# The prologue of an adaLN cross-attention kernel in a new order, with turned modulations and values placed by DMA

## The chip, the cores and the metric

The kernel runs on one core of a Trainium2 chip. The metric is the device time of one execution in microseconds (us). TensorE multiplies matrices, VectorE, ScalarE and GpSimd work elementwise, SyncE (SP) issues transfers. The engines run their own instruction streams and wait for each other by semaphores.

## The reference

```python
def _ada_ln(x, c, W_ss, b_ss):
    h = (x - mean(x)) / sqrt(var(x) + EPS)
    scale, bias = jnp.split(jax.nn.silu(c) @ W_ss + b_ss, 2, axis=-1)
    return (1.0 + scale)[:, None, :] * h + bias[:, None, :]
...
xq, xkv = _ada_ln(x_q, t_vec, Wss_q, bss_q), _ada_ln(x_kv, t_vec, Wss_kv, bss_kv)
q = (xq @ Wq + bq).reshape(B, Lq, nh, dh)          # 16 x 1024 x 512, 16 heads of 32
kv = (xkv @ Wkv + bkv).reshape(B, Lkv, 2, nh, dh)  # 64 context rows per batch
attn = softmax(q k^T / sqrt(dh));  out = attn v
return x_q + (out @ Wp + bp)
```

## The kernel before

There are 16 batches of 1024 rows; a unit is 128 rows, so there are 128 units, eight to a batch. Every matrix product is done in parts: an operand is split into a high and a low half-precision (or fp32r) part, and high x high, high x low and low x high are summed. The scales for these parts come from upper bounds, the limits, worked out at run time.

All engines run `prime()` and then `step(b, i)` for every unit, by `every_step`. A step of TensorE is score(i), turn_p(i-2), project(i+4), turn_x(i+8), project_out(i-3), weigh(i-2); the pipeline is full from the step of unit 3 on. The prologue, `prime()` and what stands ahead of it, does the work that is there only once:

- the small vectors are turned (L1025, L1027), silu of the condition is formed (L719 to L728), and `modulate` (L1032) multiplies it with Wss_kv and Wss_q, 512 columns streamed at a time; ScalarE copies the rows (L495), TensorE turns them (L1043), VectorE adds the biases (L747)
- VectorE makes statistics of the context rows (L735) and normalises them in `cx` (L755); TensorE turns them chunk by chunk (L1053), VectorE scales and shifts a chunk (L964, L967), ScalarE makes its high part (L629), GpSimd its low part (L357)
- ScalarE sums squares of the weights; `limits`, `limits_top`, `limits_copy` and `scales` (L757 to L816) make all scales from one table of 16 limits, through a transpose and a spreading product on TensorE (L1221, L1224)
- `value_rows(t)` and `key_rows(n)` (L1085, L1092) are 12 products each, eight tiles of both. A value tile's parts are formed in one go (L700 ScalarE, L833 VectorE) in `v16`, and `place` (L265) copies them to `v_all` with four copies on each engine. A key tile goes by L823, L690, L439
- `turn_x` (L1118) turns the first x tiles, which ScalarE and GpSimd have normalised (L576, L583, L370, L373, L385); Wq is scaled in four pieces (L408, L591, L951); `project` (L1135) makes the first queries, in the banks ps_q and ps_o; `bias_product` (L1106) makes the output bias; `shift_product` (L1060) the query's
- key tile 7 is made last, behind the projections. Wp's parts are made in steps 0 and 1 (L624, L937)

What sets the order is the order written in each engine's `prime()`, and the waits on semaphores in it. SP issues loads in the order of its stream and waits in it for free buffers.

## Time and profile before

| what | value |
|---|---|
| three runs | 1185.43, 1185.86, 1186.97 us, median 1185.86 |
| the profiled execution | 1185.47 us, of which the span is 1183.7 us |
| instructions | 32530 |
| busy in the span | TensorE 1140.7, VectorE 1019.2, ScalarE 858.0, GpSimd 840.1 us |
| mean granted TensorE clock | 0.986 |
| first score / fourth score start | 119.01 / 147.28 us |
| key tile 3 of 8 ends | 73.3 us |
| silu finished on VectorE | 6.04 us |
| L349 and L351 on GpSimd, four tiles' reciprocal roots | 19.43 to 20.74 us |
| a square of 128x2048 weights on ScalarE (L642) | 1.91 us |
| the limits' power on GpSimd (L445) | 1.01 us |
| scale steps L788 to L805 on VectorE | 48.42 to 50.72 us, of it 1.12 in one step of four elements |
| sums of one x tile's rows on ScalarE (L576, L583) | 1.47 us from start to start |

A profile row tells an engine's busy time, the mean of one instruction and what ended the idle time before it. TensorE instructions overlap, so the distance of two starts tells their pace better than their length. The granted clock is 1.0 at 2.4 GHz and 0.5 at 1.2 GHz.

### The profile page before, as it was taken

Reading aid. Unit: us, or ns where it says so; the run is one execution under the profiler, and the core shown is the slowest. Engines: PE = TensorE matmul, PEld = TensorE weight load, DVE = VectorE, ACT = ScalarE, POOL = GpSimd, SP = SyncE. Lnnn points to the kernel's source line nnn. Section 1 sums busy time; section 2 is a strip of 40 time slices with the busy share of each in tenths; the row PEclk is TensorE's granted clock in tenths of the full one; section 3 lists DMA queues with packets and bytes.
Section 4 is the critical chain, followed back from the end, with each engine's and each line's share of the span. In section 5 each row is a group of like instructions: output and inputs, shape, how many; then the busy total and the mean of one; then the engine's idle time right before and its main releaser. Section 6 shows DMA issues by size and latency. Waiting matters only on the chain.

```text
span 1183.7 us, 32530 instructions
## 1 busy us (share of the span) xinstructions
PE 1140.7 (96%) x11072; PEld 696.6 (59%) x11072; DVE 1019.2 (86%) x1799; ACT 858.0 (72%) x1624; POOL 840.1 (71%) x941
## 2 busy tenths in 40 slices
PE   7798699999999999999999999999999999999997
PEld 2665366566665666656666566566665666656653
DVE  4745698989989889898898988989889899898895
ACT  2477577778777777777777777777787777787653
POOL 1543486877778786868787786868687777869555
PEclk9798799999999999999999999999999999999999
DMA  8111113223223232232322323223232232232222
GB/s 331 70 36 36 63 64 100 99 90 106 89 97 106 80 106 90 96 106 80 106 92 94 106 80 106 97 89 106 81 105 97 90 106 86 100 107 65 72 73 80
DMA packets 59871, 112.00 MB, mean 95 GB/s; under 512 B 6412, under 2 KB 6440, under 8 KB 59832
## 3 DMA queue, kind: packets, MB, share of 16 engines
q1 hardware_dynamic: 59832, 111.48, 27.6%
q8 instruction: 24, 0.39, 0.1%
q14 instruction: 15, 0.12, 0.0%
HBM read 77.90 MB, written 33.55 MB: 94 GB/s over the span
## 4 chain that ended last, share of the span: by engine, by line
PE 86%; issue 2%; POOL 2%; ACT 1%; DVE 0%; POOLq 0%; ACTq 0%; DVEq 0%
PE ps_q L1135 27%; PE ps_o L1203 26%; PE ps_t L1169 11%; PE ps_v L1188 8%; PE ps_s L1154 8%; PE ps_v L1118 4%; POOL xr L418 1%; PE ps_o L1135 0%; POOL xr L394 0%; PE ps_v L1082 0%; POOL half_den L425 0%; POOL xh L385 0%; PE ps_t L1118 0%; DVE xT_lo L847 0%; ACT xT_hi L510 0%
## 5 line engine op out<-in xcount | busy, mean ns | idle before, releaser
L394 POOL TENSOR_TENSOR xr<-xr,bp_row 128x512 f32<-128x512 f32 x128 | 163.1, 1274 | 155.9 <-ACT junk L583 155.9
L885 DVE TENSOR_REDUCE mx<-ps_s 128x8 f32<-128x512 f32 x256 | 164.8, 685 | 90.8 <-PE ps_s L1154 90.4
L425 POOL TENSOR_TENSOR half_den<-pr 128x512 f32<-128x512 f32 x128 | 162.8, 1272 | 64.6 <-ACT pr L612 35.0
L558 ACT CAST pt_hi<-ps_t 128x512 f16<-128x512 f32 x256 | 137.6, 589 | 92.5 <-PE ps_t L1169 92.5
L568 ACT ACTIVATE q_hi<-ps_q,cur_bq 128x512 f16<-128x512 f32 x126 | 86.5, 687 | 133.0 <-PE ps_q L1135 110.1
L418 POOL TENSOR_TENSOR xr<-y,xr 128x512 f32<-128x512 f32 x128 | 162.4, 1269 | 6.5 <-ACT y L535 6.5
L905 DVE TENSOR_TENSOR pt_lo<-ps_t,pt_hi 128x512 f16<-128x512 f32 x256 | 163.3, 679 | 0.0
L877 DVE SCALAR_TENSOR_TENSOR pr<-pr,ps_v 128x512 f32<-128x512 f32 x256 | 162.8, 675 | 0.0
L897 DVE TENSOR_TENSOR pr<-ps_s,mx 128x512 f32<-128x512 f32 x256 | 161.9, 673 | 0.0
L612 ACT ACTIVATE pr<-pr,exp_scale 128x1024 f32<-128x1024 f32 x128 | 146.4, 1144 | 16.4 <-DVE pr L897 16.4
L1169 PE MATMUL ps_t<-ident,pr 128*128 128x128 f32 x1024 | 140.9, 281 | 4.7 <-DVE pr L877 4.7
L1203 PE MATMUL ps_o<-wp_hi,oT_hi 128*128 128x512 f16 x512 | 131.5, 379 | 6.7 <-DVE oT_lo L854 6.7
L1135 PE MATMUL ps_q<-xT_hi,w_hi 128*128 128x512 f16 x504 | 131.1, 383 | 2.1 <-DVE q_lo L915 1.8
L1203 PE MATMUL ps_o<-wp_lo,oT_hi 128*128 128x512 f16 x512 | 131.4, 379 | 0.0
L1203 PE MATMUL ps_o<-wp_hi,oT_lo 128*128 128x512 f16 x512 | 131.4, 379 | 0.0
L1135 PE MATMUL ps_q<-xT_lo,w_hi 128*128 128x512 f16 x504 | 130.6, 382 | 0.0
L1135 PE MATMUL ps_q<-xT_hi,w_lo 128*128 128x512 f16 x504 | 130.2, 381 | 0.0
L1169 PEld LDWEIGHTS ps_t<-ident,pr 128*128 128x128 f32 x1024 | 110.3, 142 | 18.4 <-DVE pr L877 5.2
L1188 PEld LDWEIGHTS ps_v<-pt_hi,vb 128*64 128x64 f16 x2048 | 82.4, 109 | 55.8 <-issue 55.8
L1154 PE MATMUL ps_s<-kb,q_hi 64*128 64x128 f16 x2048 | 108.0, 217 | 0.2 <-DVE pr L897 0.2
L1188 PE MATMUL ps_v<-pt_hi,vb 128*64 128x128 f16 x2048 | 103.0, 222 | 1.7 <-DVE xT_lo L847 1.7
L535 ACT ACTIVATE y<-ps_o,y_unscale 128x512 f32<-128x512 f32 x128 | 88.1, 688 | 18.2 <-PE ps_o L1203 14.6
(162 smaller groups left out, 2292.7 us busy)
## 6 DMA issues: line engine op xcount, KB each, us to landing
x_in<-in_x_dram SPq DMA_DIRECT2D x128, 256.0 KB, 2.7
xr<-in_x_dram SPq DMA_DIRECT2D x128, 256.0 KB, 2.9
out_dram<-xr SPq DMA_DIRECT2D x128, 256.0 KB, 2.0
raw<-in_L_xcond_Wss_kv_dram SPq DMA_DIRECT2D x4, 512.0 KB, 5.0
cx<-in_ctx_dram SPq DMA_DIRECT2D x1, 2048.0 KB, 12.1
raw<-in_L_xcond_Wss_q_dram SPq DMA_DIRECT2D x4, 512.0 KB, 12.8
raw<-in_L_xcond_Wkv_dram SPq DMA_DIRECT2D x2, 1024.0 KB, 15.9
wq<-in_L_xcond_Wq_dram SPq DMA_DIRECT2D x1, 1024.0 KB, 16.5
```

What stands on the lines that cost most here:

```text
L394: pool.tensor_tensor(xr[:, s, :], xr[:, s, :], bp_row[:, :], ALU.add).then_inc(xr_ready, 1)
L418: pool.tensor_tensor(xr[:, s, :], y[:, off % 2, :], xr[:, s, :], ALU.add).then_inc(y_ready, 1)
L425: pool.tensor_tensor(half_den[:, :, :], pr[:, off % 2, :, 0:LKV // 2], pr[:, off % 2, :, LKV // 2:LKV], ALU.add).then_inc(half_done, 1)
L877: dve.scalar_tensor_tensor(out=pr[:, off % 2, hs, :], in0=pr[:, off % 2, hs, :], scalar=P_UNIT, in1=rden[:, hs].unsqueeze(2).to_broadcast( ...
L885: dve.tensor_reduce(mx[:, HALF * h:HALF * (h + 1)], ps_s[:, h, :].rearrange("p (h l) -> p h l", l=LKV), AX_X, ALU.max)\
L897: dve.tensor_tensor(pr[:, off % 2, hs, :], ps_s[:, h, :].rearrange("p (h l) -> p h l", l=LKV), mx[:, hs].unsqueeze(2).to_broadcast([P, HAL ...
L905: dve.tensor_tensor(pt_lo[:, 4 * h:4 * h + 4, :], ps_t[:, h, :].rearrange("p (g n) -> p g n", g=4), pt_hi[:, 4 * h:4 * h + 4, :], ALU.subt ...
L1135: last = pe.matmul(bank[:, :], w[:, k, cols], xt[:, s, k, :], start=(n == 0), stop=(n == 3 * KC - 1))
L1154: last = pe.matmul(ps_s[:, e, P * m:P * (m + 1)], q[rows, s, m, cols], kb[rows, part, m, :, :].rearrange("p h l -> p (h l)"), start=(n == ...
L1169: last = pe.transpose(ps_t[:, h, P * g:P * (g + 1)], pr[:, off % 2, 2 * pair:2 * pair + 2, :].rearrange("p h l -> p (h l)"), ident[:, :])
L1188: last = pe.matmul(ps_v[64 * e:64 * (e + 1), 0, P * m:P * (m + 1)], vb[:, part, 2 * m + e, :, :].rearrange("p h c -> p (h c)"), pt[:, 4 * ...
L1203: last = pe.matmul(ps_o[:, :], ot[:, k, :], w[:, k, :], start=(n == 0), stop=(n == 3 * KC - 1))
```

## The change

- Modulation: the product is formed turned, 128x128 pieces of Wss as weights and the 16 columns of silu streamed, so that the copies L495 and the turns L1043 go. Wss_q gets a tile of its own, the loads of Wss come by columns. The first modulation follows three turned chunks; the second comes after key tile 0.
- Loads: the small vectors are issued by ScalarE's queue; SP's begin with half of the context, in two-tile pieces, then Wss_kv, Wv, the rest of the context, Wk, Wq, Wss_q, Wp, x.
- Limits: two stages of 8, one for keys and values, one for query and output, each with its transpose, spreading product and scale steps.
- Context rows 4 to 7 are normalised by GpSimd. The first four x tiles get their statistics and their rows on VectorE (`first_stats`, `first_rows`) and are turned from `x_in`.
- Values: parts are written by parity of heads, two instructions on each engine, and four DMAs per tile from SP (`place_values`) take the place of the eight copies.
- Weights' high parts are made in halves and low parts in quarters. `value_rows` and `key_rows` wait for each piece and use listed banks, partly those of the loop.
- All value and key tiles are done before the loop; three of each come after the projections.
- `step` is the same but for waits.

```diff
+            return ps_t[:, off % 2, :] if isinstance(b, int) and unit(b, off) < PER else ps_v[:, 0, :]
...
+        def chunk_bank(n):
+
+            return (ps_t[:, 0, :], ps_t[:, 1, :], ps_q[:, :])[n % TURNED]
+
+        def value_bank(t):
+
+            return (ps_s[:, 0, :], ps_s[:, 1, :], ps_v[:, 0, :], ps_v[:, 1, :], ps_v[:, 0, :], ps_t[:, 0, :],
+                    ps_t[:, 0, :], ps_o[:, :])[t]
+
+        def key_bank(n):
+
+            return (ps_s[:, 0, :], ps_s[:, 1, :], ps_v[:, 0, :], ps_v[:, 1, :], ps_v[:, 1, :], ps_t[:, 1, :],
+                    ps_t[:, 1, :], ps_o[:, :])[n]
...
+            load_context(0)
+            load_context(1)
+            load_modulation(0, Wss_kv, ld_ss)
             sp.dma_start(wv_raw, Wkv[:, H:2 * H].rearrange("(k p) n -> p k n", p=P)).then_inc(ld_wv, 16)
+            load_context(2)
+            load_context(3)
+            sp.dma_start(wk_raw, Wkv[:, 0:H].rearrange("(k p) n -> p k n", p=P)).then_inc(ld_wk, 16)
             sp.dma_start(wq[:, :, :], Wq.rearrange("(k p) n -> p k n", p=P)).then_inc(ld_wq, 16)
-            sp.dma_start(wk_raw, Wkv[:, 0:H].rearrange("(k p) n -> p k n", p=P)).then_inc(ld_wk, 16)
-            sp.dma_start(bp_row[:, :], bp.rearrange("(a n) -> a n", a=1).partition_broadcast(P)).then_inc(ld_bp, 16)
+            load_modulation(1, Wss_q, ld_ssq)
+            sp.dma_start(wp_raw, Wp.rearrange("(k p) n -> p k n", p=P)).then_inc(ld_wp, 16)
 
...
-                wait(sp, xh_ready, unit(b, off - 3))
+                if isinstance(b, int) and FIRST <= unit(b, off) < 2 * FIRST:
+                    wait(sp, xT_turned, unit(b, off - 3))
+                wait(sp, xh_ready, nth(b, off - 3))
...
+            def place_values(t):
+
+                sp.wait_ge(v_lo_done, 2 * t + 2)
+                for hb in range(2):
+                    for par in range(2):
+                        sp.dma_start(v_all[LKV * par:LKV * (par + 1), :, 2 * t + hb, :, :],
+                                     v16[LKV * hb:LKV * (hb + 1), :, t % 2, par, :]
+                                     .rearrange("p s (g d) -> p s g d", d=DH)).then_inc(v_placed[t % 2], 16)
...
+            sp.dma_start(bp_row[:, :], bp.rearrange("(a n) -> a n", a=1).partition_broadcast(P)).then_inc(ld_bp, 16)
+            for t in range(4):
+                place_values(t)
+            load_x(0, 4)
+            load_x(0, 5)
+            place_values(4)
+            for f in range(6, 12):
                 load_x(0, f)
+            for t in range(5, CT):
+                place_values(t)
...
+                context_rstd(1)
+                context_rows(4)
+                context_rows(5)
+                limits(0)
+                context_rows(6)
+                context_rows(7)
+                for n in range(KC, 2 * KC):
+                    context_lo(n)
+                key_lo(0)
+                first_rstd()
+                key_lo(1)
+                limits(1)
+                key_lo(2)
+                for m in range(KC):
+                    scaled_wq(0, m)
+                    if m == 1:
+                        key_lo(3)
+                layernorm(4)
+                layernorm(5)
+                key_lo(4)
                 layernorm(6)
                 layernorm(7)
...
+            act.dma_start(c_row, cond).then_inc(ld_small, 16)
+            for at, v, n in ((BSSQ, bss_q, 2 * KC), (BSSKV, bss_kv, 2 * KC), (BQ, bq, KC), (BK, bkv, 2 * KC)):
+                act.dma_start(brow[at:at + n, :], v.rearrange("(r c) -> r c", c=P)).then_inc(ld_small, 16)
...
-            for side in range(2):
-                act.wait_ge(mod_mm, side + 1)
-                banks = (ps_s, ps_v)[side]
-                act.copy(mod_rows[side].rearrange("b (a n) -> b a n", a=2), banks[0:B, :, :]).then_inc(mod_copied, 1)
...
+                context_hi(0)
+                value_weights_hi(0)
+                context_hi(1)
+                value_weights_hi(1)
+                context_hi(2)
+                context_hi(3)
+                sum_of_squares(wv_raw, ld_wv, 0, 1, squares[0])
+                sum_of_squares(wk_raw, ld_wk, 0, 0, squares[0])
+                key_weights_hi(0)
+                key_weights_hi(1)
+                act.wait_ge(wv_done, KC)
+                sum_of_squares(wq[:, :, :], ld_wq, 1, 0, squares[1])
+                for n in range(KC):
+                    value_hi(n)
+                    context_hi(KC + n)
+                key_hi(0)
+                sum_of_squares(wp_raw, ld_wp, 1, 1, squares[1])
+                for n in range(1, KC):
+                    key_hi(n)
+                    if n == 2:
+                        scaled_wq_hi(0, 0)
+                scaled_wq_hi(0, 1)
+                act.wait_ge(wv_done, KC)
...
-                    act.wait_ge(lim_step, SCALED_SC)
-                wait(act, v_lo_done, t - 1)
-                wait(act, v_hi_placed, t - 1)
-                act.activation(v16[0][:, t % 2, :], ps_s[:, t % 2, :], ACT.Copy, scale=v_scale[:, 0:1])\
...
-            def value_hi_place(t):
-
-                act.wait_ge(v_hi_done, t + 1)
-                place(act.copy, 0, t).then_inc(v_hi_placed, 1)
+                    act.wait_ge(kv_step, V_SCALED)
+                wait(act, v_placed[t % 2], 64 * (t // 2))
+                heads = value_bank(t).rearrange("p (g e d) -> p g e d", e=2, d=DH)
+                for par in range(2):
+                    act.activation(v16[:, 0, t % 2, par, :].rearrange("p (g d) -> p g d", d=DH), heads[:, :, par, :],
+                                   ACT.Copy, scale=v_scale[:, 0:1]).then_inc(v_hi_done, 1)
...
+                for n in range(KC):
+                    context_chunk(n)
+                    if n > 0:
+                        value_weights_lo(n - 1)
+                value_weights_lo(3)
+                context_stats(1)
+                limits(0)
+                limits_top(0)
+                key_weights_lo(0)
+                key_weights_lo(1)
+                limits_copy(0)
+                key_weights_lo(2)
+                key_value_scales()
+                key_weights_lo(3)
+                for n in range(KC):
+                    value_lo(n)
+                    context_chunk(KC + n)
+                modulation(1)
+                limits(1)
+                keys(0)
+                first_stats()
+                keys(1)
+                limits_top(1)
+                first_rows(0)
+                first_rows(1)
+                keys(2)
+                limits_copy(1)
+                first_rows(2)
+                first_rows(3)
+                query_output_scales()
+                query_bias()
+                keys(3)
+                first_wq_lo(0)
+                turned_x(0, 0)
+                first_wq_lo(1)
+                turned_x(0, 1)
+                turned_x(0, 2)
+                first_wq_lo(2)
+                turned_x(0, 3)
+                output_bias()
+                first_wq_lo(3)
+                value_lo(4)
+                query(0, 0, first_banks[0])
+                turned_x(0, 4)
+                keys(4)
+                query(0, 1, first_banks[1])
+                turned_x(0, 5)
+                query(0, 2, first_banks[0])
+                turned_x(0, 6)
+                query(0, 3, first_banks[1])
+                turned_x(0, 7)
+                for n in range(5, CT):
+                    value_lo(n)
+                    keys(n)
 
...
-                for k in range(KC):
-                    pe.wait_ge(landed[k], 16)
-                    for a in range(2):
-                        last = pe.matmul((ps_s, ps_v)[side][0:B, a, :], silu_t[:, k, :],
-                                         wss[side][:, k, H * a:H * (a + 1)], start=(k == 0), stop=(k == KC - 1))
+                dst = (ps_v[:, 1, :], ps_o[:, :])[side]
+                for m in range(2 * KC):
+                    pe.wait_ge(landed[m // 2], 16)
+                    for k in range(KC):
+                        last = pe.matmul(dst[:, B * m:B * (m + 1)], wss[side][:, k, P * m:P * (m + 1)],
+                                         silu_t[:, k, :], start=(k == 0), stop=(k == KC - 1))
                 last.then_inc(mod_mm, 1)
 
-            def turn_modulation(side):
-                pe.wait_ge(mod_copied, side + 1)
-                for m in range(2 * KC):
-                    last = pe.transpose(ps_t[:, side, B * m:B * (m + 1)], mod_rows[side][:, P * m:P * (m + 1)],
-                                        ident[0:B, 0:B])
-                last.then_inc(mod_turned, 1)
-
...
+                for n in range(TURNED):
+                    turn_context(n)
+                modulate(0, ld_ss)
+                turn_context(3)
                 value_rows(0)
...
+                value_rows(1)
+                limits_turn(0)
+                value_rows(2)
+                limits_spread(0)
+                value_rows(3)
+                for n in range(KC, 2 * KC - 1):
+                    turn_context(n)
                 key_rows(0)
...
+                pe.wait_ge(lim_copied, 1)
+                modulate(1, ld_ssq)
+                turn_context(2 * KC - 1)
+                key_rows(1)
+                pe.wait_ge(mod_ready, 4)
+                limits_turn(1)
+                key_rows(2)
+                limits_spread(1)
+                pe.wait_ge(ld_wq, 16)
+                pe.wait_ge(c_mul, CT)
+                for m in range(KC):
+                    shift_product(m)
+                key_rows(3)
+                for f in range(FIRST):
+                    turn_x(0, f)
+                value_rows(4)
+                bias_product()
+                pe.wait_ge(bq_ready, 1)
+                for m in range(KC):
+                    if m == 1:
                         pe.wait_ge(bias_ready, 1)
-                        project(0, 0, first_banks[0], 1)
-                for m in range(1, KC):
                     project(0, m, first_banks[m % 2], 1)
-                    turn_x(0, KC + m)
-                key_rows(CT - 1)
+                    turn_x(0, FIRST + m)
+                    if m == 0:
+                        key_rows(4)
+                for t in range(5, CT):
+                    value_rows(t)
+                    key_rows(t)
 
```

## Rows read from the trace of the kernel before

**Rows 1.** Stretches: busy us (and instructions) of TensorE, its loads, VectorE, ScalarE, GpSimd; clock; DMA.
```profile
0.00:26.90 26.90, 18.46 (x57) 5.34 (x57) 11.62 (x36) 4.55 (x5) 3.61 (x16) 1.00 0.88 326
26.90:52.40 25.50, 18.14 (x87) 15.46 (x88) 19.68 (x41) 13.81 (x17) 13.17 (x9) 0.73 0.33 122
52.40:119.00 66.60, 60.44 (x257) 41.39 (x255) 35.58 (x71) 47.83 (x108) 26.18 (x36) 0.95 0.11 32
119.00:147.28 28.28, 18.78 (x153) 10.35 (x153) 19.40 (x30) 15.76 (x29) 13.49 (x19) 0.76 0.20 66
```
**Rows 2.** The chain of waits in order of time: start, us, what; two scores in the loop.
```profile
147.35 0.78 PE ps_s L1154 x24
...
155.56 0.78 PE ps_s L1154 x24
```
**Rows 3.** Timeline of VectorE: start, us, line, operation: statistics and first chunks.
```profile
16.50 2.47 DVE L735 BATCH_NORM_STATS2 cst<-cx 128x6 f32<-128x512 f32 x4 [10.46 <-DMA cx<-in_ctx_dram]
...
19.16 2.44 DVE L735 BATCH_NORM_STATS2 cst<-cx 128x6 f32<-128x512 f32 x4
...
22.37 3.73 DVE L755 TENSOR_SCALAR cx<-cx,cmv,crstd 128x512 f32<-128x512 f32 x8
...
26.92 0.68 DVE L964 TENSOR_TENSOR raw<-ps_t,sc_kv 128x512 f32<-128x512 f32 x1
...
28.25 0.68 DVE L964 TENSOR_TENSOR raw<-ps_t,sc_kv 128x512 f32<-128x512 f32 x1
```
**Rows 4.** Transfers by line: size, median us from issue to landing.
```profile
raw<-in_L_xcond_Wss_kv_dram SPq DMA_DIRECT2D x4, 512.0 KB, 5.0
```
**Rows 5.** Timeline of TensorE: turned chunks and 16-column products, at either clock.
```profile
28.83 0.96 PE L1060 MATMUL ps_q<-sh_q,wq 128*128 128x16 f32 x8
29.65 0.64 PE L1053 MATMUL ps_t<-ident,cx 128*128 128x128 f32 x4
...
34.26 1.12 PE L1053 MATMUL ps_t<-ident,cx 128*128 128x128 f32 x4 [3.18 <-DVE raw L964]
35.17 1.73 PE L1060 MATMUL ps_q<-sh_q,wq 128*128 128x16 f32 x8
36.74 1.09 PE L1053 MATMUL ps_t<-ident,cx 128*128 128x128 f32 x4
```
**Rows 6.** Timeline of TensorE's weights loads, in the first modulation.
```profile
8.63 0.15 PEld L1036 LDWEIGHTS ps_s<-raw,silu_t 128*16 128x16 f32 x1 [0.70 <-issue]
9.49 0.15 PEld L1036 LDWEIGHTS ps_s<-raw,silu_t 128*16 128x16 f32 x1 [0.70 <-issue]
10.03 0.10 PEld L1036 LDWEIGHTS ps_s<-raw,silu_t 128*16 128x16 f32 x1 [0.40 <-issue]
10.46 0.10 PEld L1036 LDWEIGHTS ps_s<-raw,silu_t 128*16 128x16 f32 x1 [0.33 <-issue]
```
**Rows 7.** Groups by line up to 147.3 us: count, busy us, mean ns, idle before.
```profile
L265 ACT COPY v_all<-pt_hi 64x256 f16<-64x256 f16 x32 | 12.9, 402 | 0.3
L833 DVE SCALAR_TENSOR_TENSOR pt_lo<-ps_s,v_scale,pt_hi 128x512 f16<-128x512 f32 x8 | 6.0, 744 | 6.4 <-ACT pt_hi L700 6.4
L629 ACT CAST ctx_hi<-raw 128x512 fp32r<-128x512 f32 x8 | 4.9, 614 | 9.4 <-DVE raw L967 9.4
```
**Rows 8.** Timeline of TensorE: the start of a key tile, the output bias behind it.
```profile
55.19 1.09 PE L1082 MATMUL ps_v<-ctx_hi,wk_hi 128*128 128x512 f32 x4
...
57.98 3.60 PE L1106 MATMUL ps_o<-xr,o_slot 128*128 128x512 f32 x8
61.02 1.49 PE L1082 MATMUL ps_s<-wv_hi,ctx_hi 128*128 128x512 f32 x4
```
**Rows 9.** Timeline of TensorE while the loop's pipeline fills.
```profile
138.53 1.97 PE L1169 MATMUL ps_t<-ident,pr 128*128 128x128 f32 x8 [4.56 <-DVE pr L877]
```
**Rows 10.** Timeline of GpSimd and of VectorE, two instructions at once.
```profile
43.65 2.85 POOL L357 TENSOR_TENSOR ctx_lo<-raw,ctx_hi 128x512 fp32r<-128x512 f32 x1 [4.23 <-ACT ctx_hi L629]
...
45.60 0.92 DVE L778 TENSOR_SCALAR lim_diag<-ident,lim_top 16x16 f32<-16x16 f32 x1
```

634 lines of the change are left out of this document (315 added, 319 removed).

## The prediction

> **What bounds the kernel now.** First the stretches of the whole trace, stage by stage. TensorE is busy without a gap once the loop runs; in front of it the row of stretches shows the share it loses [rows 1]: 8.4 us of the first 26.9, 7.4 us of the next 25.5, 6.2 us of the 66.6 up to the first score, and 9.5 us of the 28.3 in which the pipeline of the loop fills. Beside the gaps stands the granted clock: 0.73 in the second stretch and 0.76 in the last. Second the chain of waits: from 146.5 us on it is TensorE alone, and a score comes every 8.21 us to the end [rows 2]. The change leaves those steps alone, so whatever it does must show as a shift of the moment at which the fourth score, score(0, 3), starts. That is 147.28 us now. All I have to work out is this moment in the new order.
>
> **Stage 1, to the end of modulation 0 (call it M), the one for keys and values.** Now the context arrives behind the weights of the modulation and its statistics start at 16.5 us; chunk 0 of the context is scaled at 26.92 us [rows 3]. In the new order the context comes first. 512 KB from the head of the queue land 5.0 us after their issue in the median [rows 4], and the vector pass over two tiles can start at about 6.3 us, once VectorE has finished the silu steps, which precede it. Four tiles of statistics take 2.66 us, as the distance of the two groups shows [rows 3]; the power on GpSimd is about 1.4 us with its waits and four normalised rows are four times 0.47 us. That puts the last of them at 12.4 us, and TensorE, idle since 4.5 us, starts the three turns there.
>
> Here I chose with care, since this is the largest term. Nothing new is computed in the modulation, but it changes shape: eight columns of four 128x128 weights loads with 16 columns streamed, instead of 512 columns streamed past a 16-column weight. The old one cannot price it. The query's shift product L1060 has exactly the new shape, 16 columns, four k. At the high clock one m takes 0.82 us (28.83 to 29.65), at the low one 1.57 us (35.17 to 36.74); a turned chunk takes 0.91 us at the low one (34.26 to 35.17) [rows 5]. So one modulation is 8 x 0.82 = 6.6 us at 2.4 GHz and 8 x 1.57 = 12.6 us at 1.2 GHz. Which clock? The clock column says 1.00 for the first stretch, but the rows say otherwise: the weights loads of the first modulation come 0.86 us apart up to 9.49 and 0.43 us apart after 10.03 [rows 6]. TensorE began at the low level although the column does not say so, and left it after 3.9 us of streaming 512 columns at a time. The stretch 34.3 to 37.8 us is made of just what the new order has at 12.4 to 27 us, turned chunks and 16-column products, and it stayed at the low level to its end [rows 5]. I take the low level for all of it: three turns end at 14.5 us (the first one is nearly finished when the last row is), plus 12.6 gives M = 27.1. Lower end: the clock rises as it did in the old modulation, some 4 us into the work, M = 21.6. What the new form removes, the two ScalarE copies of 1.0 us and the second transposes, is paid for by this: chunk 0 starts at 27.1 + 0.35 = 27.5 us against 26.92.
>
> **Stage 2, to the end of key tile 3 (K3).** TensorE waits for others here, so I followed the hand-written order on all engines; times are counted from M.
>
> Each chunk takes VectorE 1.33 us [rows 3], ScalarE's high part 0.61 [rows 7]. Four chunks with the halves and quarters of the value weights between them end at M+7.4, the last low part on GpSimd at M+9.4. Value tile 0 then ends at M+11.9 and tile 1, half of it at the low clock, at M+15.2; a tile is 2.79 us at the high clock [rows 8].
>
> The first limit waits for two squares on ScalarE (M+12.0) and for tile 1; TensorE's order puts tile 2 between turning and spreading. Spread at M+18.4, power 1.0, the six steps and v_scale 1.9: M+21.3.
>
> Then ScalarE and VectorE alternate: high part of a value tile 0.8, low part 0.8, chunk 1.36, its high part 0.55, none beside another: 3.55 us x 4 (halves cost a little more than the 0.74 us of a whole [rows 7]), and 0.6 us for chunk 7, whose turn is queued behind the second modulation on TensorE: M+36.1.
>
> keys(0), its high part and the square of Wp put the second limit at M+40.8, 4.7 later. Key tile 2, the spread (0.3), four 16-column products (3.3) and key tile 3: M+50.0. The change adds waits on SP: loads of x tiles 4 to 11 stand behind placements. ScalarE asks for x tile 4 some 8 us after its load lands, and value_hi(2) asks for the place of tile 0 some 6 us after its low part, for four issues and a landing of about 4.5; both are covered, and cost up to 3 us if a placement took twice that.
>
> To this I add 0.8 us for the port that VectorE and GpSimd share, bounded below. K3 = 27.1 + 50.8 = 77.9. Now key tile 3 ends at 73.3.
>
> **Stage 3, K3 to the first score.** Left are four value and four key tiles (8 x 2.78 = 22.2), the output bias 3.05 us [rows 8], four projections at 2.6 (10.4) and eight turned x tiles at 0.4 (3.3): 39.0 us. The four x tiles turn in two banks and each waits for VectorE and ScalarE between the pieces of Wq: 5.0 us idle, value tile 4 then runs mostly at the low clock, 1.6 more, and key tile 7 shares ps_o with value tile 7 and waits 1.5 us for its low part. 39.0 + 8.0 = 47.0; first score at 124.9, now 119.0. What leaves ScalarE (placing: 32 copies, 12.9 us [rows 7]) does not shorten this, as TensorE is the one that is late in it.
>
> **Stage 4, filling.** Unchanged code, but ScalarE, VectorE and GpSimd come to it less burdened: now q_hi of the fifth query waits for x rows of GpSimd, which stood behind key_lo(7). With that gone project(0, 5) comes 1.5 us and the first normalised tile 2.4 us earlier. TensorE's wait of 4.56 us before it [rows 9] stays in kind, since wp_hi and wp_lo are still in the way. 28.3 - 2.4 = 25.9.
>
> **Sum.** 124.9 + 25.9 = 150.8 against 147.28: +3.5 us. The profiled execution took 1185.47 us (1183.7 of span and 1.8 around it), 0.4 below the median 1185.86. 1185.5 + 3.5 = **1189.0 us**.
>
> **Rivals.** First, *the clock rises in the modulation.* M = 21.6; the rest follows it, as nothing in stage 2 waits for a load. 5.5 us less: 1183.5 us. For it: the old modulation did rise. Against: it streamed 512 columns, and the turned chunks and 16-column products at 34.3 us did not. The Trainium skill, TensorE: Matmul & The Clock Gate, PE-mode transpose, adds that transposes do not count as activity for the gate; no run here shows them alone. Chance 0.2.
>
> Second, *it works as a reordering should.* The clock rises, and stage 3 runs warm with the turned x tiles hidden: 5.5, and 5 of the 8 us lost in stage 3: 1178.5 us. For it: 12.9 us of copies leave ScalarE, and four tiles' row sums, 1.5 us each. Against: the written order, which chains x tiles to pieces of Wq. Chance 0.15.
>
> Third, *GpSimd in the way of VectorE.* The new order moves four context rows onto GpSimd, next to the limit steps and weights parts on VectorE. The row of GpSimd at 43.65 took 2.85 us where its like took 1.27 without company, and VectorE's 16-element step that began at 45.60 lasted 0.92 us until it ended [rows 10]. If every one of the eight low parts and four rows costs 0.5 to 1.6 us on the chained path and the clock falls inside the second modulation too, that is 5 us more: 1194 us. It decides once two such steps in each of the four rounds collide. The Trainium skill, SBUF — State Buffer, Who interferes with whom, makes it a lock held for a whole instruction whenever VectorE has two SBUF inputs; every second step of a chunk has. Bounded: 0 below (no meeting), 6 above; I took 0.8. Chance 0.15.
>
> **Numbers.** Forecast 0.5 (its own range 1186 to 1193), of which about 0.15 lies within 0.2% of the median, 1183.5 to 1188.2 us, about what a measurement can tell from no change. Rival 1 is half in that band, half below. Faster 0.1 + 0.15 = 0.25, same 0.15 + 0.1 = 0.25, slower 0.35 + 0.15 = 0.5. The range 1180 to 1195 leaves out the lower half of rival 2 and the upper third of rival 3, with the ends of the forecast's own.
>
> **What would show it.** Modulation 0 between 14.5 and 27 us with weights loads twice as far apart as after the clock has risen; its rows 0.1 us apart instead of 0.2 would mean rival 1. chunk 0 at 27.5, last chunk at 63, key tile 3 done at 78, first score at 125, fourth at 151, loop steps still 8.21 us. The prediction is wrong if loop steps change, or if TensorE does not wait for VectorE between 31 and 68 us.

## The result, and the profile after

The changed kernel takes 1201.92 us in the median (1199.72 to 1204.59), the kernel before in the same comparison 1186.41: ratio 1.0131, interval 1.0108 to 1.0154, 15.5 us slower. The forecast was 1189.0, range 1180 to 1195: the sign holds, the size doesn't, and the time lies outside the range. The profiled execution took 1199.72 us, its span 1197.9. It is the fastest of the four, so the traces below explain 14.2 of the 15.5 us.

First the chain of waits after, two scores in the loop (start, us, what), then the stretches of the trace, cut where the prediction's four stages end (columns as in [rows 1]):

```profile
161.57 0.78 PE ps_s L1323 x24
...
169.78 0.78 PE ps_s L1323 x24
```

```profile
0.00:32.30 32.30, 17.61 (x81) 16.69 (x81) 6.65 (x20) 1.54 (x2) 2.30 (x15) 1.00 0.99 342
32.30:88.90 56.60, 46.22 (x218) 37.76 (x219) 38.64 (x92) 21.89 (x32) 29.05 (x23) 0.91 0.11 33
88.90:136.80 47.90, 41.79 (x185) 28.60 (x183) 17.89 (x29) 22.63 (x50) 15.30 (x22) 0.96 0.22 65
136.80:161.50 24.70, 15.47 (x153) 9.67 (x152) 19.16 (x30) 17.08 (x32) 12.02 (x16) 0.86 0.23 78
```

A score still comes every 8.21 us [rows 2]. The fourth starts 14.2 us later than before (161.5, was 147.3), and from it to the end of the span it is 1036.4 us in both kernels, and within 0.2 us of that in each one below. So a kernel can be judged by the start of its fourth score, and the stages can be set against the sum:

| stage | forecast | after |
|---|---|---|
| 1, to the end of modulation 0 (M) | 27.1 | 32.3 |
| 2, M to the end of key tile 3 | 50.8 | 56.6 |
| 3, to the first score | 47.0 | 47.9 |
| 4, first to fourth score | 25.9 | 24.7 |

Stages 3 and 4 are right within 1.2 us. TensorE's timeline after shows what became of the first two (in brackets the idle time before, and what ended it):

```profile
8.15 0.28 PE L1160 MATMUL ps_t<-ident,o_slot 28*128 28x28 f32 x1 [8.15 <-DMA o_slot<-in_L_xcond_bkv_dram]
...
15.34 2.61 PE L1182 MATMUL ps_t<-ident,cx 128*128 128x128 f32 x8 [6.51 <-DVE cx L841]
...
18.59 13.67 PE L1172 MATMUL ps_v<-silu_t,raw 128*128 128x16 f32 x64
...
58.45 0.33 PE L1182 MATMUL ps_t<-ident,cx 128*128 128x128 f32 x1 [1.91 <-POOL cx L401]
...
62.28 8.74 PE L1172 MATMUL ps_o<-silu_t,wss_q_raw 128*128 128x16 f32 x64
70.86 1.09 PE L1182 MATMUL ps_t<-ident,cx 128*128 128x128 f32 x4
71.61 2.06 PE L1253 MATMUL ps_s<-ctx_hi,wk_hi 128*128 128x512 f32 x4
...
77.50 0.27 PE L1197 MATMUL ps_o<-ident,lim 128*8 128x128 f32 x1 [1.54 <-issue]
...
80.90 3.75 PE L1189 MATMUL ps_q<-sh_q,wq 128*128 128x16 f32 x32
84.49 1.84 PE L1253 MATMUL ps_v<-ctx_hi,wk_hi 128*128 128x512 f32 x4
```

The first row: the small vectors are there at 8.15 us, before it was 3.7, and TensorE is idle until then. Modulation 0 takes 13.67 us, all at the low level: 0.21 us a product, where eight products with the clock up take 0.81 us (62.84 to 63.65 in a7 below). Behind value tile 3 a turn waits 1.91 us for a row of GpSimd; modulation 1 and the shift products end with the clock down, and key tiles 1 and 3 (71.61, 84.49) begin at 1.2 GHz, as 2.06 and 1.84 us for four products show where 1.1 is the length at the high clock [rows 8]. The turn of the second limit (77.50) starts when the square of Wp is finished on ScalarE:

```profile
75.40 1.91 ACT L572 ACTIVATE raw<-xr 128x2048 f32<-128x2048 f32 x1
77.21 0.19 ACT L572 ACTIVATION_READ_ACCUMULATOR raw<-xr 128x1 f32 x1
```

GpSimd's timeline after, the context rows that it took over:

```profile
46.70 4.16 POOL L401 TENSOR_SCALAR cx<-cx,cmv,crstd 128x512 f32<-128x512 f32 x2
...
54.08 4.31 POOL L401 TENSOR_SCALAR cx<-cx,cmv,crstd 128x512 f32<-128x512 f32 x2
```

And the alternation behind them, on ScalarE and on VectorE: a high part of a chunk, two halves of a value tile, then the low halves and the next chunk, 3.6 us a round:

```profile
60.26 0.62 ACT L708 CAST ctx_hi<-raw 128x512 fp32r<-128x512 f32 x1 [3.48 <-DVE raw L1074]
60.79 0.83 ACT L791 ACTIVATE v<-ps_s,v_scale 128x256 f16<-128x256 f32 x2
63.89 0.62 ACT L708 CAST ctx_hi<-raw 128x512 fp32r<-128x512 f32 x1 [2.27 <-DVE raw L1074]
```

```profile
61.65 0.88 DVE L929 SCALAR_TENSOR_TENSOR v<-ps_s,v_scale,v 128x256 f16<-128x256 f32 x2 [1.43 <-ACT v L791]
62.45 0.68 DVE L1071 TENSOR_TENSOR raw<-ps_q,sc_kv 128x512 f32<-128x512 f32 x1
63.16 0.69 DVE L1074 TENSOR_TENSOR raw<-raw,sh_kv 128x512 f32<-128x512 f32 x1
```

The first chunks show one thing more. While GpSimd makes low parts (first line, the next one from 39.52 on), VectorE's steps with both inputs in SBUF take 1.37, 1.03 and 1.31 us where the same steps take 0.68 or 0.69 without company:

```profile
34.84 3.40 POOL L415 TENSOR_TENSOR ctx_lo<-raw,ctx_hi 128x512 fp32r<-128x512 f32 x2 [20.22 <-ACT ctx_hi L708]
35.74 1.37 DVE L1078 TENSOR_TENSOR wv_lo<-raw,wv_hi 128x512 fp32r<-128x512 f32 x1 [0.30 <-ACT wv_hi L713]
37.75 1.03 DVE L1074 TENSOR_TENSOR raw<-raw,sh_kv 128x512 f32<-128x512 f32 x1
40.02 1.31 DVE L1074 TENSOR_TENSOR raw<-raw,sh_kv 128x512 f32<-128x512 f32 x1
```

### The profile page after: what moved, and what is told of

It reads as the page before. It is cut to its first block, busy times and chain, and to the rows that moved or that the text cites. A ratio compares the mean times of both kernels' runs of the same rounds, so it can differ in the third digit from the quotient of the medians.

```text
span 1197.9 us, 32905 instructions
## 1 busy us (share of the span) xinstructions
PE 1146.0 (96%) x11155; PEld 716.9 (60%) x11155; DVE 1015.4 (85%) x1796; ACT 839.9 (70%) x1584; POOL 844.6 (71%) x937
## 4 chain that ended last, share of the span: by engine, by line
PE 83%; issue 3%; POOL 1%; DVE 0%; ACT 0%; POOLq 0%; DVEq 0%
PE ps_q L1302 26%; PE ps_o L1372 26%; PE ps_t L1339 10%; PE ps_v L1356 8%; PE ps_s L1323 8%; PE ps_v L1285 4%; POOL xr L476 1%; POOL xr L452 0%; POOL half_den L483 0%; ACT wp_hi L703 0%; DVE mx L993 0%; POOLq L42 0%; DVE den L970 0%; DVE pr L1005 0%; ACT pr L692 0%
## 5 line engine op out<-in xcount | busy, mean ns | idle before, releaser
L610 ACT ACTIVATE y<-ps_o,unscale 128x512 f32<-128x512 f32 x128 | 88.2, 689 | 18.2 <-PE ps_o L1372 14.9
## 6 DMA issues: line engine op xcount, KB each, us to landing
raw<-in_L_xcond_Wkv_dram SPq DMA_DIRECT2D x2, 1024.0 KB, 11.4
wss_q_raw<-in_L_xcond_Wss_q_dram SPq DMA_DIRECT2D x4, 512.0 KB, 11.4
```

## The experiments

Kernels are called by the first part of their names (a1, b2): those with an a start from the changed kernel, those with a b from the kernel before. The median of the kernel before lay between 1185.1 and 1186.4 us in the comparisons; the ratio stands with each kernel. "Fourth score" is of its profiled execution.

**One term of the new kernel at a time.** a1, small vectors at the head of SP's stream again:

```diff
-            act.dma_start(c_row, cond).then_inc(ld_small, 16)   # and brow, on ScalarE's queue
+            sp.dma_start(c_row, cond).then_inc(ld_small, 16)    # and brow, ahead of load_context(0)
```

> The changed kernel with one edit: the five small vectors go back to the head of SP's stream, in front of the context. Theory (the loss is a sum of waits on one chain through the prologue): the vectors landed at 8.15 us where they landed at 3.7 before, silu, statistics and all behind them shift by that; the fourth score, at 161.5 us in the changed kernel, comes at about 157.3, 4.2 us earlier, and the time falls by as much. Rival (slack behind it: the loads of Wss_kv or the weights squares set the next waits): less than 1 us, fourth score at 160.5 or later.

Measured: 1197.25 us, 1.0102 (1.0083 to 1.0120). Vectors at 3.78, modulation 0 from 14.30 to 27.98: the 4.3 us came. The fourth score of the profile came only 2.5 earlier (159.0), since modulation 1 now took 9.5 us and the tiles behind it more of the low clock.

a3, context rows 4 to 7 on VectorE instead of GpSimd:

```diff
-                context_rows(4) ... context_rows(7)     # pool
+                for t in range(4, CT): dve.tensor_scalar(cx[:, t, :], ...)   # behind limits(0)
```

> The changed kernel with context rows 4 to 7 normalised by VectorE behind the first limits, not by GpSimd. Theory (GpSimd needs 2.1 us for a row where it took 0.77 for an x row before, and chunk 4 waits 2.2 us for them): chunk 4 no longer waits, VectorE spends 1.9 us more in a stretch where it waits for the limit anyway; fourth score at about 159.5, 2 us earlier. Rival (the rows ran beside other waits): within 0.5 us of 161.5.

Measured: 1200.82 us, 1.0136 (1.0119 to 1.0154). Chunks 4 to 6 turn without a wait and key tile 0 starts at 57.55 instead of 59.4, but modulation 1 then takes 9.88 us instead of 8.74, and the fourth score comes at 160.4: nothing that the times can tell. The row itself was mis-sized: 2.08 us on GpSimd, where its like, with an addition in place of the subtraction, takes 0.89 in the mean in the kernel before. VectorE was idle from 45.8 to 49.7 us, over most of the first pair, so for this pair it isn't the meeting of the two engines on their shared port.

a2, products of 512 columns on junk ahead of the turns and of modulation 0, to raise the clock first:

```diff
+            warm(12)        # before the small vectors
+            warm(26)        # before pe.wait_ge(silu_step, 3)
```

> The changed kernel with 12 and 26 extra matmuls of 512 columns into an unused bank, ahead of the small turns and ahead of the first turned chunks, where TensorE waits anyway. Theory (modulation 0 took 13.7 us because TensorE was at 1.2 GHz): it runs like modulation 1, 8.7 us, and the three turned chunks in 1.6 instead of 3.2; 6.4 us earlier by its end, fourth score at about 155.5. Rival (the form is bound by its weights loads at either clock): modulation 0 stays above 12 us, fourth score at 160 or later.

Measured: 1199.74 us, 1.0121 (1.0098 to 1.0145). Modulation 0 took 10.79 us, not 13.67, and key tile 0 started 4.9 us earlier; modulation 1 then took 11.15 us and the fourth score came at 162.3, 0.8 later than without. The gain up to key tile 0 was given back.

a4, chunk 7's turn ahead of modulation 1:

```diff
+                turn_context(2 * KC - 1)
                 modulate(1, ld_ssq)
-                turn_context(2 * KC - 1)
```

> The changed kernel with chunk 7 turned ahead of modulation 1 instead of behind it. Theory: VectorE's wait of 2.2 us for that chunk goes, but the end of modulation 1 comes 0.5 us later and key tile 1 behind it; the second limit waits for the square of Wp, which follows chunk 7's high part and keys(0), so it comes 2 us earlier; fourth score at about 159.7. Rival (TensorE's key tile 1, not the chunk, sets the second limit): 161.5, no change.

Measured: 1201.17 us, 1.0136 (1.0109 to 1.0163), no gain: limit 2 is turned at 77.1 us (77.5 after), so chunk 7 wasn't what it waited for.

**Is it TensorE's work at all?** a6, modulation 1 with one of its four k, so that three quarters of its sum are left out:

```diff
-                    for k in range(KC):
+                    for k in range(KC if side == 0 else 1):
...
```

> The new kernel with modulation 1 cut to one of its four k: 8 products instead of 32, so three quarters of its sum are left out. It took 8.74 us, so 6.5 us of TensorE's work go, and nothing is moved. Theory one, TensorE is the bound from value tile 1 to key tile 3, with products of 16 columns that lose it the clock: chunk 7 no longer waits 2.2 us for its turn, and limit 2, shift products and key tile 3 come 5 to 6 us earlier, with key tile 1 at the high clock. First score at 131.5 instead of 136.8, time 1196. Theory two, the alternation of ScalarE and VectorE with GpSimd's rows is the bound and TensorE only follows: only chunk 7's wait of 2.2 us goes, first score at 134.6, time 1199.7 or more.

Measured: 1201.01 us, 1.0133 (1.0115 to 1.0151). 6.9 us of work are gone and nothing is gained. Its timeline of TensorE says where they went:

```profile
62.80 1.85 PE L1172 MATMUL ps_o<-silu_t,wss_q_raw 128*128 128x16 f32 x16
...
74.16 0.37 PE L1197 MATMUL ps_o<-ident,lim 128*8 128x128 f32 x1 [6.22 <-ACT raw L572]
74.28 2.04 PE L1253 MATMUL ps_v<-ctx_hi,wk_hi 128*128 128x512 f32 x4
```

TensorE waits 6.22 us for L572, the square of Wp, which ScalarE does behind the alternation, and comes out of the wait at the low clock: key tile 2, the shift products and key tile 3 take 15.1 us instead of 11.3. The limit is turned 3.3 us earlier than with all four k (74.16, was 77.50), and the clock takes 3.8 back. Both theories expected a gain; both missed this wait.

a7, filling: a product of 512 columns behind each m of modulation 1 and ahead of each shift product:

```diff
+                    for _ in range(1 if side else 0):
+                        pe.matmul(ps_s[:, 1, :], wk_hi[:, 0, 0:P], wk_hi[:, 0, :], start=True, stop=True)
...
+                pe.wait_ge(v_lo_done, 4)        # ahead of modulation 1; a like wait ahead of the shift products
```

> The new kernel with one product of 512 columns (0.23 us at the high clock) behind each m of modulation 1 and ahead of each m of the shift product, into banks that are free: 12 products, 2.8 us of added work, whose results nobody reads. If it is the 16-column form that lets TensorE's clock fall in these places: modulation 1 takes 6.6 + 1.9 = 8.5 us at the high clock, as long as now, key tile 1, the shift products and key tile 3 keep the high clock (3.3 + 0.9 and 2.8 us, now 3.7 and 4.4), and key tile 3 ends 1 to 2 us earlier: time 1200.5. If the clock falls in any case (from waits, or from what went before), the filling is simply added: key tile 3 2.8 us later or more, time 1204.7.

Measured: 1205.67 us, 1.0166 (1.0139 to 1.0192). The filling is simply added. The clock still fell inside modulation 1, from 0.81 us for eight products (62.84 to 63.65) to 1.57 (70.23 to 71.80).

**The parts put into the kernel before, alone.** b1, turned modulations:

```diff
+                for m in range(2 * KC):
+                    pe.wait_ge(landed[m // 2], 16)
+                    for k in range(KC):
+                        last = pe.matmul(dst[:, 0, B * m:B * (m + 1)], wss[side][:, k, P * m:P * (m + 1)], silu_t[:, k, :], ...)
-            turn_modulation(0)      # and (1), with ScalarE's copies
```

> The kernel before with the turned form of both modulations alone (and their weights loaded by columns); the two copies on ScalarE and the second transposes go, the order stays. Theory one, the form costs what the new kernel shows: 12.6 to 13.7 us at the low clock for modulation 0 from 6.1 us on, to 19.5 instead of 14.9, and modulation 1 follows at 9 to 12.6 us, to 28.5 to 32 instead of 24.9. Chunk 0 is scaled 3 to 6 us later (now 26.92), fourth score 2 to 5 us later than 147.3: time 1188 to 1190. Theory two, the form is neutral, since its transposes and copies are saved: modulation 0 ends at 16, modulation 1 at 25, time 1185.1 within 1 us, or less.

Measured: 1191.88 us, 1.0054 (1.0037 to 1.0071). TensorE's timeline of this kernel:

```profile
6.33 13.81 PE L1036 MATMUL ps_s<-silu_t,raw 128*128 128x16 f32 x64 [1.93 <-DMA raw<-in_L_xcond_Wss_kv_dram]
19.97 13.81 PE L1036 MATMUL ps_v<-silu_t,raw 128*128 128x16 f32 x64
```

Both stay at the low level for 27.4 us without a gap, where the streamed form had left it after 3.9 us [rows 6]; the first chunk is turned at 33.6 instead of 24.8, the fourth score comes 6.2 later. The form costs 5.9 us in this kernel.

b2, values placed by DMA:

```diff
-                    value_hi_place(t)       # ScalarE; VectorE's value_lo_place(t) too
+            for t in range(CT):             # SP
+                place_values(t)
+                load_x(0, 4 + t)
```

> The kernel before with its values placed by DMA alone: the 32 copies of ScalarE (12.9 us) and as many of VectorE go, value tiles are written in two halves by parity, the placing DMAs stand in SP's queue between the loads of x tiles 4 to 11. Theory one, ScalarE paces the rounds of one value and one key tile (6.4 us a round against 5.9 us of TensorE's work): eight rounds become 0.4 us shorter each, first score at 115.8 instead of 119.0, time 1182. Theory two, TensorE has no slack to give or the x tiles behind the placements come late: first score within 1 us of 119.0, time 1185, at worst 1187.

Measured: 1180.0 us, 0.9953 (0.9937 to 0.9969). This part of the change is worth 6 us there. A round of a value and a key tile takes 6.00 us (69.36 to 75.36 on TensorE), 6.37 before, so eight rounds give 3.0 us, which is what theory one asked for. The trace shows where more comes from: behind the third projection the kernel before waited 3.31 us for an x row and ran the fourth at the low clock, 5.0 us for the 2.6 of the others; with the values placed by DMA the two waits there are 1.64 and 2.33 us, and the projection keeps the high clock. The lines are of the kernel before:

```profile
109.81 1.12 PE L1118 MATMUL ps_t<-ident,xh 128*128 128x128 f32 x4 [3.31 <-POOL xh L385]
110.72 1.91 PE L1135 MATMUL ps_o<-xT_hi,w_hi 128*128 128x512 f16 x4
```

**Back from the new kernel.** a9, both modulations in the old form:

```diff
+                for k in range(KC):
+                    pe.wait_ge(landed[k], 16)
+                    for a in range(2):
+                        last = pe.matmul(dst[a], silu_t[:, k, :], wss[side][:, k, H * a:H * (a + 1)], ...)
...
+                turn_modulation(0)
```

> The new kernel with both modulations in the old form (512 columns streamed past a 16-column weight, rows copied by ScalarE, turned back on TensorE), weights loaded by rows, everything else as it is. Modulation 0 takes 8.8 + 1.1 + 0.7 = 10.6 us as in the kernel before, not 13.7, and modulation 1 7.0 us at the high clock plus a copy and a turn behind chunk 7's turn. Theory one, the turned form costs the new kernel what it cost the kernel before (5.9 us): time 1196. Theory two, the 3 us gained up to modulation 0 are given back by the clock and by the second limit's chain behind them: 1200 to 1201.5.

Measured: 1196.69 us, 1.0086 (1.0065 to 1.0106): 5.2 us back, near the same price from the other side. Modulation 1 in this form kept the high clock to its end (eight rows of 0.86 us from 59.09 on), in the place where the turned one loses it.

a10, small vectors first, and the second half's statistics and rows on VectorE while it waits for modulation 0; a11, the same with streamed modulations:

```diff
+            context_stats(1)
+            dve.wait_ge(c_pool, 4)
+            for t in range(4, CT): dve.tensor_scalar(cx[:, t, :], ...)
             modulation(0)
```

> The new kernel with the small vectors first, and with the statistics and the rows of context tiles 4 to 7 all on VectorE in its idle time under modulation 0 (15.7 us idle there), instead of behind chunk 3 and on GpSimd. Turned modulations stay. It takes 2.8 us of VectorE and 8.5 us of GpSimd out of the stretch between tile 0 and chunk 4. Theory one, that stretch is bound by VectorE and GpSimd: chunk 4's turn does not wait, key tile 0 starts at M + 24 instead of M + 27, fourth score near 155, time 1193. Theory two, the alternation of ScalarE and VectorE with values 0 to 3, and the clock behind it, decide: fourth score at 158 to 159, time 1196.5 to 1198, as with the small vectors alone.

> The two before in one: small vectors first, second half early on VectorE, modulations streamed. If the terms add: 4.3 us of the small vectors, 3 of the modulation, 2 to 3 of the rows, 9 to 10 us less than the new kernel, time 1191.5. If most is given back: 1196. If it falls under 1186 the order of the two limits and of values and keys in front costs nothing of its own.

Measured: 1196.07 us, 1.0087 (1.0066 to 1.0107), and 1190.3 us, 1.0036 (1.0024 to 1.0048). With the form repaired the two are worth 6.4 us (1196.69 to 1190.3); without it the second part adds 1.2 us to the small vectors alone, which is within the noise. 10.3 us against the kernel with placed values alone were left.

The profile of a10 looks like its theory one (fourth score 154.7, 1192.87 us), but it is of an execution 2.4 us faster than the next of the other three (1195.29 to 1196.87). In it modulation 0 took 10.57 us: its products run at 10 to 12 a us from 14 to 18 us and at 6 to 7 a us behind that, where a1 has 6 to 7 a us all the way. TensorE had done nothing but turns until then:

```profile
11.00 2.60 PE L1176 MATMUL ps_t<-ident,cx 128*128 128x128 f32 x8 [6.52 <-DVE cx L831]
13.40 1.06 PE L1176 MATMUL ps_q<-ident,cx 128*128 128x128 f32 x4
14.25 10.57 PE L1166 MATMUL ps_v<-silu_t,raw 128*128 128x16 f32 x64
```

**What is left.** From a11: the x tiles' turns spread between other work (a12); modulation 1 ahead of value tile 0 (a13); both (a14).

```diff
                 turn_x(0, 0)
                 turn_x(0, 1)
+                value_rows(4)
                 turn_x(0, 2)
+                bias_product()
                 turn_x(0, 3)
```

```diff
                 turn_context(3)
+                modulate(1, ld_ssq)
                 value_rows(0)
+                turn_modulation(1)
```

> The kernel with small vectors first, second half early and streamed modulations (1190.3 us), with one more edit on TensorE alone: value tile 4 between the turns of x tiles 1 and 2, the output bias between 2 and 3, instead of all four turns one after the other. There TensorE was idle 3.7 us and then ran value tile 4 at the low clock (78.1 to 89.2 us for 5.6 us of work at the high one). Theory one, this wait and its clock are a real part of what is left: 3.5 to 5 us less, 1186. Theory two, the pieces of Wq and the x tiles on VectorE and ScalarE pace the stretch anyway: turn 2 and the projections wait instead, within 1 us of 1190.3.

> The same kernel (1190.3 us) with modulation 1 and its turn moved from behind key tile 0 to where the kernel before has it in kind, under TensorE's waits: ahead of value tile 0, whose fourth chunk is not there anyway; Wss_q is loaded ahead of the key weights for it. Theory one, behind key tile 0 TensorE is the bound, and the 7.8 us of it are free in front of value tile 0, where it is idle 5.9 us: key tile 3 ends 6 us earlier, time 1184.5. Theory two, the squares and the second limit on ScalarE and VectorE decide (with three quarters of modulation 1 left out nothing was gained): 1189 to 1190.

> Both of these moves in one. If both terms are real and add: 1180.5 us. If the first limit now comes later, as modulation 1 delays value tile 0 and 1, 1185.

Measured: 1189.97 us, 1.0039 (1.0022 to 1.0055); 1191.85, 1.0060 (1.0038 to 1.0082); 1191.23, 1.0050 (1.0034 to 1.0066). None gained. In the first the wait moved on: 0.95 before turn 2, 1.45 before the first projection, 1.94 for the first x row of GpSimd. The second is a6 again in the trace, more clearly:

```profile
54.10 1.10 PE L1264 MATMUL ps_s<-ctx_hi,wk_lo 128*128 128x512 f32 x4
64.34 0.37 PE L1208 MATMUL ps_o<-ident,lim 128*8 128x128 f32 x1 [9.14 <-ACT raw L563]
64.47 2.05 PE L1264 MATMUL ps_v<-ctx_hi,wk_hi 128*128 128x512 f32 x4
```

So TensorE's 7.0 us of modulation 1 are no longer ahead of the limit, and the limit is turned only 0.8 us earlier (64.34, 65.11 in a11): the alternation with the square behind it sets the pace. a15, two edits on ScalarE alone, on top of a13:

```diff
                 sum_of_squares(wq[:, :, :], ld_wq, 1, 0, squares[1])
+                sum_of_squares(wp_raw, ld_wp, 1, 1, squares[1])
+                value_hi(0)
                 for n in range(KC):
-                    value_hi(n)
+                    if n < KC - 1:
+                        value_hi(n + 1)
                     context_hi(KC + n)
```

> The kernel with modulation 1 early (1191.9 us), with two edits on ScalarE alone: the square of Wp ahead of the first value tile, where ScalarE is idle 3.6 us, and the high part of value tile n+1 ahead of chunk n+4's, so that ScalarE works while VectorE does the low part and the chunk. There the two alternate, 3.62 us a round, of which ScalarE is idle 2.27 and VectorE 1.43, TensorE then idle 9.14 us for the square of Wp and at the low clock for 15 us behind it. Theory one, this alternation is the bound of the stretch up to key tile 3, which is why no term of TensorE's showed: rounds of 2.3 us, limit 2 turned at 56 instead of 64.3, key tile 3 done at 71 instead of 79.6, time 1184. Theory two, GpSimd's parts or the banks of TensorE hold the rounds at 3.6 us, or the clock takes the gain: 1189 to 1192.

Measured: 1185.88 us, 0.9999 (0.9990 to 1.0008), 6 us less. Its timeline of ScalarE, and TensorE at limit 2:

```profile
47.50 1.57 ACT L792 ACTIVATE v<-ps_s,v_scale 128x256 f16<-128x256 f32 x4 [1.50 <-DVE v_scale L903]
50.61 0.62 ACT L699 CAST ctx_hi<-raw 128x512 fp32r<-128x512 f32 x1 [1.54 <-DVE raw L1080]
53.41 0.84 ACT L792 ACTIVATE v<-ps_v,v_scale 128x256 f16<-128x256 f32 x2 [2.18 <-DMA v_all<-v]
```

```profile
59.72 0.37 PE L1210 MATMUL ps_o<-ident,lim 128*8 128x128 f32 x1 [4.11 <-DVE lim L862]
```

Limit 2 is turned 4.6 us earlier, and now waits for VectorE and no longer for the square. The two edits were not tried one at a time, so their shares are not known. It didn't reach the 56 us expected, as ScalarE now waits 2.18 us for the placing DMA of value tile 0 to free its slot, and 1.26 us for that of tile 1 (56.02): what frees ScalarE in the kernel before holds it here.

**An early context in the old forms.** b4: b2, with the first half of the context loaded ahead of the weights, its chunks scaled right behind modulation 0, one limit as before:

```diff
             modulate(0, ld_ss)
             turn_modulation(0)
+            for n in range(KC):
+                turn_context(n)
             modulate(1, ld_ssq)
```

> The kernel before with values placed by DMA, and with what the change wanted from an early context, but in the old forms: first half of the context loaded ahead of the modulation's weights, its four chunks turned and scaled right behind modulation 0, modulation 1 (still streamed) behind them, one limit as before, key tile 0 in front of the spread. Theory one, the start of the chunks is what the prologue hangs on: value tile 0 at 34 to 35 us instead of 39.5, v_scale at 43 instead of 50, two tiles done by then, fourth score 8 us earlier than in the kernel with placed values alone (142.7): time 1172. Theory two, a later load or the clock takes it back: 1178 to 1180.

Measured: 1189.76 us, 1.0035 (1.0024 to 1.0045), a miss by 18 us: TensorE waited 4.46 us for second-half rows and then ran the shift products, 6.85 us at the low clock, ahead of value tile 0 (46.3 instead of 34), and waited 4.12 us more ahead of value tile 2. Mended in two steps: in b5, rows of both halves ahead of modulation 0 and the shift products behind value tile 1, in b6, a piece of Wq out of GpSimd's way:

```diff
-                    if KC < n < KC + 3:
-                        scaled_wq(0, n - KC - 1)
+                    if n == KC + 1:
+                        scaled_wq(0, 0)     # scaled_wq(0, 1) follows in the value rounds
```

> The kernel with an early context in the old forms, mended where it went wrong (1189.8 us): there TensorE waited 4.46 us for rows of the second half and ran 6.9 us of shift products at the low clock ahead of value tile 0, and ScalarE waited 15.6 us for a piece of Wq ahead of the first values. Now all rows are normalised under modulation 0, the shift products stand behind value tile 1, and the pieces of Wq behind the first values. Theory one: value tile 0 at 35 us, v_scale at 45 instead of 50, fourth score near 136, time 1174. Theory two, one limit for everything holds the values back whatever comes early: 1179 to 1181.

> The kernel with an early context in the old forms (1186.05 us), mended once more: the second piece of Wq is scaled on GpSimd in the value rounds and no longer ahead of the low part of chunk 7, where GpSimd waited 11.3 us for VectorE, and with it TensorE 4.5 us for the first x tile, behind which value tile 3 ran at the low clock. Until that wait it was 3.5 us ahead of the kernel with placed values alone (third key tile done at 65.5 instead of 69.0 us). Theory one, that lead is now kept: fourth score at 139 to 140 us instead of 142.7, time 1177. Theory two, the lead goes in the next wait or in the clock: 1180 to 1182.

Measured: 1186.05 us, 1.0000 (0.9990 to 1.0010), then 1177.19 us, 0.9933 (0.9920 to 0.9947). The last is the fastest of all: 8.8 us under the kernel before, 24.7 under the changed one. In the step between, GpSimd had waited 11.3 us for VectorE with the low part of chunk 7 behind it, TensorE 4.5 us for an x row, and the next value tile ran at the low clock. In the two profiles the fourth score moves by 7.3 us (148.6 to 141.3): 4.5 us of wait and, behind it, 8.9 us for a turn and two tiles that take 6.0 at the high clock. The medians differ by 8.9.

## Why the prediction was right or wrong

**What held.** The loop was not touched; the fourth score carries the whole difference. Stage 3, 47.0 forecast, 47.9 measured, with the idle time behind x tile 1 (3.70 us) and the wait of key tile 7 (1.84) where they were put. Stage 4, 25.9 forecast, 24.7 measured. Modulation 0 stayed at 1.2 GHz in this trace though the clock column reads 1.00. The alternation was priced at 3.55 us a round and runs at 3.62, and the square of Wp is what limit 2 waits for, as the prediction said.

**Rival 1** did not happen in the profiled execution, but it can: a10's traced execution had the high clock in the first 4 us of modulation 0. What the prediction put against it from the Trainium skill, TensorE: Matmul & The Clock Gate, PE-mode transpose, is not borne out by this trace: the high level came behind turns alone.

**Stage 1, the start of the chain.** The step said that silu is ready at 6.0 us as before and statistics start at 6.3. But the change had moved the small vectors to ScalarE's queue, where they compete with the context and the weights from SP: 8.15 us, silu at 10.5. The three turns end at 18.6 instead of 14.5, which is 4.1 of the 5.2 us; in a1 they end at 14.3. This step failed: the prediction gave the change of the issuing queue no price. The Trainium skill, DMA: Bandwidth & Descriptors, Issuing engines are not separate DMA queues, says that transfers of different engines run on the same 16 DMA engines and interleave; the trace agrees, 8.15 against 3.78 us with the same vectors at the head of the one stream. The other 1.1 us are the size of the modulation, 13.67 for 12.6: the term was 8 x 1.57 us, and one m in a long run took 1.71.

**The form.** Its sign was argued rightly from [rows 5] and [rows 6]: the form stayed at the low level for 13.7 us on end in a1 and for 27.4 in b1, and in the traced execution of a10 it fell back to it after 4 us. Its price stood in the sum only through M; b1 and a9 put it at 5.9 and 5.2 us.

**Stage 2, the second failed step.** The chain was the right one; four of its terms were too small. The sum had the first four chunks scaled at M+7.4, v_scale at M+21.3, chunk 7 at M+36.1, limit 2 at M+40.8 and key tile 3 at M+50.0. They came at M+9.1, M+23.6, M+41.1, M+45.2 and M+56.6:

- up to v_scale 2.3 us too little, of which 1.7 are in the first chunks: VectorE's steps beside GpSimd's low parts (0.69, 0.34 and 0.62 us longer, lines above)
- the rounds, 17.5 us instead of 14.8. Chunk 4's turn comes late, as GpSimd's rows take 2.08 us each, and the first round takes 4.9 us; chunk 7 waits 2.2 us for its turn behind modulation 1 (8.74 us, the clock falling at its end), taken as 0.6
- from chunk 7 to limit 2, 4.1 us instead of 4.7
- from limit 2 to key tile 3, 11.4 us instead of 9.2: the sum had the high clock there, but the shift products and key tile 3 run partly at the low one. The 0.8 us added for the port stand against all this.

Taking one such term out gives little, though (a3, a4, a6), and the sum shows no sign of that: a term of TensorE's is hidden beside the alternation, and a wait of TensorE that comes in its place is followed by the low clock. a15 shows it from the other side: two edits on ScalarE alone give 6 us.

**Placing by DMA.** The prediction said that what leaves ScalarE does not shorten stage 3, as TensorE is the late one there. For the new order that may be so; no run here undoes this part in it. The wait for a free slot, which the prediction called covered, doesn't show in the changed kernel; in a15, where ScalarE comes back sooner, it is 2.18 and 1.26 us. As a part of the change it is the best one, 6.0 us in the kernel before (b2). It was never set against the others, because the sum went along the new order alone.

**The account of the 15.5 us.** Placing -6.0 (b2); turned form +5.2 (a9) to +5.9 (b1); small vectors on the second queue with the late second half +6.4 (a9 to a11); alternation and square of Wp 6.0 (a13 to a15). Together some 12 us; by this account 3.5 are left. Between a15 (1185.9) and b2 (1180.0) it is 5.9, mostly since a13 had itself cost 1.5 us over a11. They are the rest of the new order: the trace of a15 still has 3.70 us idle behind x tile 1 and value tile 4 at the low clock behind it, but a12, which broke up that wait in a11, gained nothing (0.95, 1.45 and 1.94 us in its place). What exactly holds them stays open. The terms don't add exactly, since the clock changes with each.

**Rival 3** happened in part. VectorE and GpSimd did get in each other's way on the chain: 1.7 us in the first chunks, and 0.39 in a scale step (L880 at 54.31 took 0.55 us, the same step in a3 0.16), where the sum had 0.8. But the slow context rows were slow by themselves, with VectorE idle beside the first pair. The Trainium skill, SBUF — State Buffer, Who interferes with whom, speaks of instructions of both at once; the first chunks agree with it, and it can't explain a row that is slow alone. Rival 3's time, 1194, was the nearest of those given.

## What to carry to other kernels

When a prologue is rewritten, find for each stretch which chain ends last, and expect little from a term outside it. If two engines alternate, try to let one of them run a step ahead: here that, together with the square of Wp moved, gave 6 us where three moves on TensorE gave nothing. Price every instruction that changes its queue, DMAs of a few KB too, and every matmul whose shape changes, at the clock that its new neighbours will leave it. Put the parts of a change into the old kernel one at a time: here one part alone was worth 6 us, and was buried under the rest. Look at how the profiled execution's time lies among the others before its trace is taken for the kernel's.

## What was not expected of the hardware

- A wait costs TensorE its length and something behind it, but not in proportion. Behind the wait of 4.50 us in b5 the work takes 2.9 us more than in b6, behind that of 3.31 in the kernel before 2.8 more than at the high clock. Behind 6.22 us in a6 and 9.14 in a13 (where most of the next 15.2 us is at the low clock) it takes 3.8 and 3.9 us more than the same work after, behind a wait of 1.54.
- In modulation 1 the clock fell with TensorE busy without a gap, after and in a7; in a9, with the streamed form in the same place, it stayed up.
- When the clock rises isn't set by TensorE's instructions alone. With the same ones from 14.3 us on, modulation 0 took 13.68 us in a1 and 10.57 in a10; the streamed modulation 0 took from 7.14 us (a13) to 9.95 (b2, against 8.82 in the kernel before, with the same instructions). A difference of 2 or 3 us between two single profiles can be this alone. One execution each of a4 and a7 (1198.27 and 1201.97 us) is 2.8 and 2.4 us below the next one; that they are of the same kind is likely, but they were not traced.
- A GpSimd row of 128x512 with two per-partition scalars takes 2.08 us as (x - a) * b and 0.77 to 0.89 as (x + a) * b. The two also differ in where the scalars lie, so the operation isn't proven to be the cause.
